# Attention over 16 images: the order of the outputs changed, and the setup rearranged

## The reference, cut to what matters

```python
xn = group_norm(x, gamma, beta)               # 32 groups, over an image's 1024 tokens
xf = xn.reshape(B, N, C)                      # B 16, N 1024, C 512
q = xf @ wq + bq
k = xf @ wk + bk
v = xf @ wv + bv
scores = jnp.einsum('bnc,bmc->bnm', q, k) * C ** (-0.5)
attn = jax.nn.softmax(scores, axis=-1)
out = jnp.einsum('bnm,bmc->bnc', attn, v)
out = out @ wp + bp
return out.reshape(B, H, W, C) + residual     # residual is x
```

## Time and profile before

| | |
|---|---|
| median of three runs | 2138.52 us |
| the profiled execution | 2139.97 us, of it 2138.3 us from the first to the last instruction |
| PE busy | 2099.0 us (98%) |
| DVE busy | 1798.7 us (84%) |
| POOL busy | 877.3 us (41%) |
| ACT busy | 743.7 us (35%) |
| one image inside the loop | 129.78 us |

### The profile page before, as it was taken

The page is one execution under the profiler, slowest core; times in us unless marked ns, Lnnn a source line. Parts: engine busy times, 40 slices in busy tenths (PEclk is TensorE's granted clock), DMA queues, the critical chain, the costliest instruction groups (busy, mean ns, idle before and its releaser), DMA issues.

```text
span 2138.3 us, 28427 instructions
## 1 busy us (share of the span) xinstructions
PE 2099.0 (98%) x9253; PEld 1730.9 (81%) x9253; DVE 1798.7 (84%) x2554; ACT 743.7 (35%) x1216; POOL 877.3 (41%) x475
## 2 busy tenths in 40 slices
PE   7999999999999999999999999999999999999999
PEld 5877888888888888888888788888878888888887
DVE  6898897988979888888888979889788898888865
ACT  4242332423333243332523324233332433335232
POOL 2452442524335244443524425243352434435253
PEclk9999999999999999999999999999999999999999
DMA  8003012030300203012030120303012030120101
GB/s 211 20 11 109 1 54 64 15 103 0 94 24 34 83 0 118 0 49 69 10 108 0 56 62 15 103 0 93 25 34 83 0 118 0 49 69 10 69 1 60
DMA packets 110268, 108.13 MB, mean 51 GB/s; under 512 B 8476, under 2 KB 74016, under 8 KB 110240
## 3 DMA queue, kind: packets, MB, share of 16 engines
q1 hardware_dynamic: 107984, 103.58, 16.0%
q10 hardware_dynamic: 2256, 4.20, 0.8%
HBM read 74.19 MB, written 33.55 MB: 50 GB/s over the span
## 4 chain that ended last, share of the span: by engine, by line
PE 51%; DVE 19%; issue 18%; POOL 7%; ACT 3%; DMA 0%; POOLq 0%; DVEq 0%; ACTq 0%
PE psum L1226 6%; PE psum L1228 6%; PE psum L1227 6%; PE psum L1251 5%; PE psum L1253 5%; PE psum L1252 5%; PE psum L1140 4%; PE psum L1139 4%; PE psum L1137 4%; DVE pt_lo L694 4%; POOL total_part L449 4%; DVE score L869 3%; DVE xn_lo L694 3%; POOL total_part L458 2%; PE psum L1057 2%
## 5 line engine op out<-in xcount | busy, mean ns | idle before, releaser
L1251 PE MATMUL psum<-v_hi,pt_hi 128*128 128x512 f32 x1024 | 401.4, 392 | 20.6 <-DVE pt_lo L694 17.4
L426 POOL TENSOR_TENSOR x_res<-x_res,out_bias 128x512 f32<-128x512 f32 x128 | 201.8, 1600 | 499.1 <-PE psum L1140 371.4
L1252 PE MATMUL psum<-v_lo,pt_hi 128*128 128x512 f32 x1024 | 399.2, 390 | 0.0
L1253 PE MATMUL psum<-v_hi,pt_lo 128*128 128x512 f32 x1024 | 399.0, 390 | 0.0
L694 DVE TENSOR_TENSOR pt_lo<-score,pt_hi 128x512 fp32r<-128x512 f32 x256 | 295.2, 1178 | 28.3 <-POOL total_part L449 25.0
L449 POOL TENSOR_TENSOR total_part<-total_part,score 128x512 f32<-128x512 f32 x192 | 309.1, 1610 | 16.6
L592 ACT ACTIVATE score<-psum 128x512 f32<-128x512 f32 x256 | 152.5, 596 | 342.3 <-PE psum L1228 341.9
L1251 PEld LDWEIGHTS psum<-v_hi,pt_hi 128*128 128x128 f32 x1024 | 192.6, 188 | 68.5 <-DVE pt_lo L694 25.1
L1253 PEld LDWEIGHTS psum<-v_hi,pt_lo 128*128 128x128 f32 x1024 | 192.6, 188 | 40.3
L1252 PEld LDWEIGHTS psum<-v_lo,pt_hi 128*128 128x128 f32 x1024 | 192.7, 188 | 39.1
L1226 PE MATMUL psum<-v_hi,xn_hi 128*128 128x512 f32 x512 | 201.7, 394 | 0.0
(11 more groups left out here) (162 smaller groups left out, 3992.2 us busy)
## 6 DMA issues: line engine op xcount, KB each, us to landing
x_res<-in_x_dram SPq DMA_DIRECT2D x128, 256.0 KB, 3.0
out_dram<-x_res SPq DMA_DIRECT2D x128, 256.0 KB, 2.2
x_blk<-in_x_dram SPq DMA_DIRECT2D x240, 128.0 KB, 3.2
score<-in_x_dram SPq DMA_DIRECT2D x16, 128.0 KB, 8.0
w_q<-in_L_conv_wq_dram SPq DMA_DIRECT2D x1, 1024.0 KB, 5.5
w_k<-in_L_conv_wk_dram SPq DMA_DIRECT2D x1, 1024.0 KB, 7.9
w_v<-in_L_conv_wv_dram ACTq DMA_DIRECT2D x1, 1024.0 KB, 9.1
w_p<-in_L_conv_wp_dram ACTq DMA_DIRECT2D x1, 1024.0 KB, 13.0
```

Of the source, the lines that this page charges most:

```text
L426: last = nc.gpsimd.tensor_tensor(at, at, out_bias[:, first:end], ALU.add)
L1251: nc.tensor.matmul(dst, hi[:, m, queries], v_hi[:, m, :], start=m == 0, stop=False)
L1252: nc.tensor.matmul(dst, hi[:, m, queries], v_lo[:, m, :], start=False, stop=False)
L1253: end = nc.tensor.matmul(dst, lo[:, m, queries], v_hi[:, m, :], start=False, stop=m == NT - 1)
```

## The change

It has three parts, and it computes the same.

**The order of the outputs** (DVE, each image). The diagonal and reciprocal of the first half (`totals(b, 0)`) move from before the last lo part of the values to behind `shifts(b, 1)`. The loop over j no longer has the lo part of the next image's xn between the lo parts of the exponentials: it makes two lo parts and then output j, and all four `xn_lo_parts` follow. `variance(b + 1)` moves up from behind the last maximum to behind the seventh.

**Image 0.** POOL no longer adds the residual of tiles 0 to 3 (`first_residual` on DVE does it), and the lo parts of the four block sums move from behind the norm of image 1 to between the last four outputs; PE waits for them in the queries of image 1.

**Setup.** The loads of wv and wp are issued when wq has arrived, before ACT's first splits. The last quarter of image 0 is transposed ahead of wv's lo part. The variance comes ahead of two lo parts and of the bias sums (`sum_products`), which now stand between the lo parts of m. POOL's block sums stand behind the power and wait for the first half of xn; ACT splits them after the first queries. The first queries of image 0 use PSUM banks 0 to 3 in order (`first_bank(h, j)`), so that the first two needn't wait for the lo part of m.

```diff
-        def first_bank(j):
-            return work[(2 + j) % 4]
+        def first_bank(h, j):
+            return work[(2 * h + j) % 4]
...
             pool.wait_ge(s_seth, SET_A_LAST + 1)
+            root(0)
+
+            pool.wait_ge(s_xl0, KC)
             block_sum(S1, a21, a22, ALU.add)
...
             block_sum(S4, a12, ab_sum[:, S2], ALU.subtract)
-            root(0)
...
                 top(b, 1)
-                if starts(b):
-                    for i in range(TH):
-                        residual(b, i)
                 totals(b, 1)
...
-            setup_hi_parts(SET_WQ, wq_t_hi)
+
+            act.wait_ge(s_wload[0], 16)
             load_rows(act, wv, w_v, s_wload[2])
             load_rows(act, wp, w_p, s_wload[3])
+            setup_hi_parts(SET_WQ, wq_t_hi)
...
-                act.wait_ge(s_as, len(SUMS))
-            for at in SUMS:
-                nc.scalar.activation(ab_hi[:, at], ab_sum[:, at], ACT.Copy).then_inc(s_abh, 1)
...
+                    act.wait_ge(s_as, len(SUMS))
+                    for at in SUMS:
+                        nc.scalar.activation(ab_hi[:, at], ab_sum[:, at], ACT.Copy).then_inc(s_abh, 1)
                 v_hi_part(b, 0)
...
+            def first_residual(i):
+
+                dve.wait_ge(s_bias, BIAS_STEPS)
+                dve.wait_ge(s_xr[i], 16)
+                at = x_res[:, i, :]
+                nc.vector.tensor_tensor(at, at, out_bias[:], ALU.add).then_inc(s_res, 1)
...
-            for n, (at, c, r) in enumerate(WHOLE):
+            for n, (at, c, r) in enumerate(WHOLE[:2]):
                 block_lo(at, n + 1, whole_block(c, r))
             group_variance(0)
-            dve.wait_ge(s_wide, 16 * 3)
-            dve.wait_ge(s_again[0], 16 * NI)
-            sum_products(0, KC)
+            for n, (at, c, r) in enumerate(WHOLE[2:]):
+                block_lo(at, n + 3, whole_block(c, r))
             variance(0)
...
-            setup_lo_parts(SET_M, m_hi, m_lo)
+            setup_lo_parts(SET_M, m_hi, m_lo, 0, 2)
+            dve.wait_ge(s_wide, 16 * 3)
+            dve.wait_ge(s_again[0], 16 * NI)
+            sum_products(0, KC)
+            setup_lo_parts(SET_M, m_hi, m_lo, 2, KC)
...
+                    if more and m == 6:
+                        variance(b + 1)
...
-                if more:
-                    variance(b + 1)
...
-                    if starts(b) and m == 4:
-                        for n, at in enumerate(SUMS):
-                            block_lo(at, len(WHOLE) + n + 1, ab_sum[:, at])
-                totals(b, 0)
                 v_lo_part(b, NT - 1)
                 tile_shift(b, 1)
                 shifts(b, 1, 0, NT)
-                tile_out(b, 0)
+                totals(b, 0)
+                if starts(b):
+                    for i in range(TH):
+                        first_residual(i)
+
                 for j in range(KC):
                     pt_lo_parts(b, 1, 2 * j, 2 * j + 2)
-                    if more:
-                        xn_lo_parts(b + 1, j, j + 1)
-                    if j:
-                        tile_out(b, j)
+                    tile_out(b, j)
+                if more:
+                    xn_lo_parts(b + 1, 0, KC)
...
                         sum_lo_part(b + 1, i - TH)
+                    if starts(b):
+                        block_lo(SUMS[i - TH], len(WHOLE) + i - TH + 1, ab_sum[:, SUMS[i - TH]])
...
+                        pe.wait_ge(s_abl, len(WHOLE) + len(SUMS))
                         pe.wait_ge(s_xsl, earlier(n) * 4 + 1)
                     block_product(BANK_6, S2, p, xs_hi, xs_lo, 1, 1)
```

More of the change, by code:

```diff
@@ L567, in first_query_hi @@
                 act.wait_ge(s_first, h * KC + j + 1)
-                nc.scalar.activation(t_hi[h][:, j, :], first_bank(j), ACT.Identity, bias=wk_bq[:, j:j + 1]).then_inc(s_th, 1)
+                nc.scalar.activation(t_hi[h][:, j, :], first_bank(h, j), ACT.Identity, bias=wk_bq[:, j:j + 1]).then_inc(s_th, 1)
             def queries(n):
@@ L619, in second_split @@
                     nc.scalar.activation(xn_hi[:, k, BANK:N], x_t[:, 1, k, :], ACT.Copy).then_inc(s_xh, 1)
-            setup_hi_parts(SET_WQ, wq_t_hi)
+            act.wait_ge(s_wload[0], 16)
             load_rows(act, wv, w_v, s_wload[2])
             load_rows(act, wp, w_p, s_wload[3])
+            setup_hi_parts(SET_WQ, wq_t_hi)
             setup_hi_parts(SET_WK, wk_t_hi)
-            setup_hi_parts(SET_A, a_full, 0, KC - 1)
-            setup_hi_parts(SET_WV, wv_t_hi)
+            setup_hi_parts(SET_A, a_full, 0, KC - 2)
             act.wait_ge(s_wload[3], 16)
@@ L629, in _ @@
                 nc.scalar.activation(wp_hi[:, k, :], w_p[:, k, :], ACT.Copy).then_inc(s_wph, 1)
+            setup_hi_parts(SET_A, a_full, KC - 2, KC - 1)
+            setup_hi_parts(SET_WV, wv_t_hi)
             setup_hi_parts(SET_A_LAST - (KC - 1), a_full, KC - 1, KC)
@@ L798, in first_query_lo @@
                 dve.wait_ge(s_th, h * KC + j + 1)
-                nc.vector.scalar_tensor_tensor(out=t_lo[h][:, j, :], in0=first_bank(j), scalar=wk_bq[:, j:j + 1],
+                nc.vector.scalar_tensor_tensor(out=t_lo[h][:, j, :], in0=first_bank(h, j), scalar=wk_bq[:, j:j + 1],
                                                in1=t_hi[h][:, j, :].bitcast(FP32), op0=ALU.add,
@@ L942, in _ @@
             quarter_transpose(0, 2)
+            quarter_transpose(0, 3)
             setup_lo_parts(SET_WV, wv_t_hi, wv_t_lo)
-            quarter_transpose(0, 3)
             token_stats(0, 1, 0, KC)
@@ L1104, in work_bank @@
                 elif what in (("v", 0, 0), ("v", 0, 1)) and starts(n):
-                    pe.wait_ge(s_tl, 3 + what[2])
+                    pe.wait_ge(s_tl, 1 + what[2])
                 elif not (before and starts(n)):
@@ L1187, in first_queries @@
                     if h and j < 2:
-                        pe.wait_ge(s_tl, j + 1)
+                        pe.wait_ge(s_tl, j + 3)
                     elif h:
                         pe.wait_ge(s_free, j - 1)
+                    elif j == 2:
+                        pe.wait_ge(s_setr, lo_rank(SET_M) + 1)
+                    elif j == 3:
+                        pe.wait_ge(s_setr, lo_rank(SET_M) + 2)
                     elif j == 1:
-                        pe.wait_ge(s_setr, lo_rank(SET_M) + 2)
-                    elif j == 0:
-                        pe.wait_ge(s_setr, lo_rank(SET_M) + 1)
+                        pe.wait_ge(s_seth, SET_A_LAST + 1)
                     for k in range(KC):
@@ L1206, in first_queries @@
                         hi, lo = (part[:, k % 2, chunk(j % 2)] for part in block_parts(at))
-                        nc.tensor.matmul(first_bank(j), hi, xn_hi[:, k, tokens], start=k == 0, stop=False)
-                        nc.tensor.matmul(first_bank(j), hi, xn_lo[:, k, tokens], start=False, stop=False)
-                        last = nc.tensor.matmul(first_bank(j), lo, xn_hi[:, k, tokens], start=False, stop=k == KC - 1)
+                        nc.tensor.matmul(first_bank(h, j), hi, xn_hi[:, k, tokens], start=k == 0, stop=False)
+                        nc.tensor.matmul(first_bank(h, j), hi, xn_lo[:, k, tokens], start=False, stop=False)
+                        last = nc.tensor.matmul(first_bank(h, j), lo, xn_hi[:, k, tokens], start=False, stop=k == KC - 1)
                     last.then_inc(s_first, 1)
@@ L1302, in _ @@
                 image(0, True)
-                pe.wait_ge(s_abl, len(WHOLE) + len(SUMS))
             if B > 2:
```

## The result

The changed kernel took 2226.78 us (median of four runs, 2223.4 to 2229.24), the kernel before 2138.64 us beside it (median of four too; one of its executions took 3012.9 us). The ratio is 1.0412, with a 95% interval from 1.0397 to 1.0426: 4.1% slower, where 2220 us or 3.8% had been forecast. The profiled execution of the change took 2223.4 us, 2221.7 of them its span.

A forecast was written before the change was run, and what follows sets the result against it. PE, busy 98% of the span, was taken as the bound, with DVE's chain setting the changed loop's length: 2139.97 + 84 (loop) + 2.3 (image 0) - 5.3 (setup) = 2221.0 us, less 1.45: 2220 us, 3.8% slower; range 2185 to 2250.

The forecast's parts named there:

- The configuring instruction: POOL, second half in the loop: comes 0.2 us after the late reciprocal, the addition 6.8 to 7.3 us after it.
- the smaller sum: Loop total with the skill's 6 us code load: delay 5.5 us instead of 6.6, the sum some 15 us smaller.
- Rival (a): POOL's 7 us run from the reduction's end whatever waits between, so no delay: 2121 us; chance 0.09.
- The loop's size: Fourteen images, each 6.0 us longer (5.4 to 7.1) through DVE's chain: +84 us, from 76 to 99.
- rival (d): The delay holds and PE's waits also lower its clock in every image, 1.9 us each: 2247 us; chance 0.12.
- the middle term: DVE's chain from POOL's addition to the next image's `v_lo`: 0.5 us longer, from 0.2 to 1.3.
- only reordered: The formerly interleaved part of DVE's chain was taken as no shorter; with output 0 now inside, 0.5 us was added.
- The norm: DVE in the loop: the earlier reduction runs beside a norm step, so the norm ends 1.9 us later.
- would give: Loop without the delay: the new order gains 1.05 us an image, 14.7 for 14 images; not subtracted from the forecast.
- rival (b): No delay, but the norm step is held until the reduction ends; the loop gains nothing: 2136 us; chance 0.03.
- Setup and image 0: Setup -5.3 us (-10 to 0), from waits gone less work given back; image 0 +2.3 us (0 to +4).
- at half of that excess: Setup: POOL's eight bias-chain steps slowed beside DVE, 1.66 us instead of 0.69 at worst; half taken, 4.4 us given back.

The follow-up runs named there:

- e11: Changed kernel with the two waits ahead of POOL's first addition swapped, the exponential's first, nothing added: 2134.12 us, ratio 0.9967.
- e10: Changed kernel plus a tiny POOL addition behind the wait for the reciprocal, with a second wait for something long over: 2226.97 us, ratio 1.04.
- e1: Changed kernel with the first half's diagonal and reciprocal put back ahead of the last lo part of the values: 2130.71 us, ratio 0.996.
- e8: Changed kernel with nine more query products on PE in each image from 1 on, ahead of the fourth, where PE waited: 2208.56 us, ratio 1.0323.
- e4: Changed kernel with outputs, reciprocal and variance in their old order, leaving only the setup and image 0 edits: 2131.05 us, ratio 0.9961.
- e2: Changed kernel plus a tiny POOL addition (128 x 4) between the second half's reduction and the wait for the reciprocal: 2134.42 us, ratio 0.9979.
- e5: Changed kernel, reciprocal still late, with only the next image's variance put back behind the last maximum: 2229.76 us, ratio 1.0425.

## Why the prediction was right, point by point

**The configuring instruction.** It was forecast at 0.2 us behind the reciprocal and came there. The load was put at 6.8 to 7.3 us, and was 6.9. The pause of POOL was forecast as 16 us and was 15.62, that of DVE as 8 and was 8.56. The Trainium skill's 6 us for the first call behind a `ModifyPoolConfig` ("GPSIMD Engine Reference", "Instruction dispatch") fits in kind; here the first addition of the total came 6.7 to 7.7 us behind its configuring instruction in the loop (7.0 in the middle), and the rows decided rightly against the smaller sum. Rival (a), no delay at all, fell: the same compiled steps gave 15.6 us or 8.6 by the place of the wait (the change, e11), and e10 has 15.6 again.

**The loop's size.** Forecast +6.0 us an image, 84 in all. Measured from the third value tile of image 1 to that of image 15: 1904.96 us instead of 1817.07, so 87.9, or 6.28 an image. The forecast summed up DVE's chain. The parts as PE shows them were partly others:

| in an image | forecast | measured |
|---|---|---|
| output tile 0 waits for `v_lo` | 0.3 | 1.5 |
| output tile 4, `pt_lo`, more than the 1.4 before | 2.6 | 1.1 |
| queries, `v_lo` | 2.6 | 2.3 |
| lower clock behind that, mean | only in rival (d) | 1.3 |

The measured ones are the gaps between products in image 3 beyond the usual 0.227 us, the restart of 0.1 included, and the clock's 1.5 us in 12 images of 14. They make 6.2. The forecast's own parts make 5.5, half a us short of its 6.0. The wait in the queries stands ahead of the fourth query product; the prediction called it the third.

The 6.0 itself came from DVE's chain, and images 4 and 14, where the clock stayed up, show what that chain cost alone:

| term | forecast | measured, images 3 and 4 |
|---|---|---|
| POOL's addition later | 6.6 | 6.7 |
| DVE's work from there to the next `v_lo` | +0.5 | -0.6 |
| slack ahead of that `v_lo` | -1.1 | -1.2 |
| image longer, clock up | 6.0 | 5.0 (134.82 and 134.91 us, less 129.79) |

So the middle term was mis-sized, and the chain by itself came out under the lower bound of 5.4. The prediction took the `xn_lo` for "only reordered". In the kernel before, two of the four stood beside POOL's additions and took 2.31 us each; in the change all four come behind them and take 4.62 together, 2.2 us saved, against 0.8 more for the `pt_lo`, 0.7 for output 0 and 0.1 for the row term (before, then the change):

```profile
546.71 2.31 DVE L694 TENSOR_TENSOR xn_lo<-x_t,xn_hi 128x1024 fp32r<-128x1024 f32 x1
...
559.88 1.22 DVE L694 TENSOR_TENSOR xn_lo<-x_t,xn_hi 128x1024 fp32r<-128x1024 f32 x1
```

```profile
572.15 4.62 DVE L696 TENSOR_TENSOR xn_lo<-x_t,xn_hi 128x1024 fp32r<-128x1024 f32 x4
```

**The norm.** This step was mis-sized. It was to lose 1.9 us beside the reduction, by the one step of the earlier trace rows; it lost 3.2 (6.16 instead of 2.98), as three of the four steps were hit (2.77, 1.29 and 1.52 us instead of 0.81). The first reduction came 2.2 us sooner, not 1.8 (10.9 us behind PE's third value tile instead of 13.1), and the second fell into the norm as well. So the gain that the loop "would give", 1.05 us an image, was 0.1 (e1), though the sum didn't use it. Output tile 0 then waited as rival (b) had it, 1.2 us (1.5 with the restart). By its rule, for which the prediction named the Trainium skill ("SBUF — State Buffer", "Who interferes with whom"), a norm step is held until the reduction has ended. The trace doesn't agree: the second step, beside the first reduction from its start, ended at 538.64 and the reduction at 539.32, much as in the earlier trace rows, and the fourth ran from 539.78 to 541.30, wholly inside the maximum's reduction (539.24 to 541.97).

**The clock.** Rival (d), with a chance of 0.12 and 1.9 us an image, was in part what happened: 1.5 us in 12 images, 18 us (e8). The prediction gave the clock nothing in the loop. That the size of the loop came out right (6.28 for 6.0) is luck: the clock's 1.3 us an image, left out of the sum, and the 1.0 us by which DVE's chain was put too long nearly cancelled. The mechanism, the late configuring instruction, is not luck: each of its signs came as forecast.

**Setup and image 0.** PE starts the first scores at 70.98 instead of 77.23 us: 6.25 gained, 5.3 forecast. (The eight steps "at half of that excess" are 3.9 us and not 4.4, so the forecast's own terms give 5.8. The eleven experiments with this setup start the first scores between 70.33 and 72.50 us.) From there to the scores of image 1 it takes 137.40 us instead of 135.59: 1.8 lost, 2.3 forecast. The wait for `ab_lo` was 5.2 us for 6, and the clock fell behind it. The four residual steps on DVE took 5.80 us together, 1.8 each but for the first, beside POOL's additions. e4 puts both parts together at -8 us. It has the residual steps and the late lo parts of the sums too, but the old order of the outputs, and its image 0 is 2.3 us shorter than before: so the loss of image 0 comes with the new order.

**The sum.** 2138.3 + 87.9 - 6.25 + 1.8 = 2221.7 us, the span. The profiled execution was 3.4 us under the median of its runs; the one before was 1.3 over its own. Instead of taking 1.45 us off, 3.4 had to be added: 4.8 of the 6.8 us by which the forecast is short.

## What to carry to other kernels

Where an engine must load code before its next step, look at what stands ahead of the configuring instruction in the compiled order: a wait there turns a load that hid beside other work into a load behind it. Of several waits before a step, put the one that ends last next to the step (or give it a step of its own), and read in the compiled order whether it is then attached behind the load; here swapping two lines was worth 93 us. And a move that gives one engine its result earlier must be followed to what it then meets: here the variance, with its reductions 2.2 us sooner, brought a reduction into the norm and cost all that the new order had won.

## What the runs showed of the hardware

**The load has a price of its own in each direction.** Behind its configuring instruction a plain step came after about 7 us whatever its size (128 x 4 in e2: 6.8 to 7.6 us in 16 cases, 7.1 in the middle; 128 x 512, line 449, in the loop of the change: 6.7 to 7.7, 7.0 in the middle). A reduction came sooner, after 5.5 to 6.4 us, 5.7 in the middle (46 cases in the change).

**The clock falls behind quite short waits, not always.** In the change, 2.1 us without a product in the queries were followed by the lower clock in 12 images of 14 and not in two, with waits of the same length (2.05 us in image 3, 2.12 in image 4). In e10, with waits as long, it fell in all 14, in e5 in 12, but there images 8 and 11 were spared and not 4 and 14. In e1, where the loop's only waits from image 2 on are the 1.2 us at output tile 0, the clock stayed at 1.00 there. A wait of 1.6 us in the setup (before 31.70 us in e1, before 31.87 in the change) was followed by the lower clock in e1 and not in the change, the same products on either side:

```profile
30.00:38.00 8.00, 6.45 (x24) 5.13 (x24) 4.59 (x15) 1.20 (x2) 1.00 (x1) 0.79 0.91 197
```

```profile
30.00:38.00 8.00, 6.38 (x31) 5.14 (x30) 5.96 (x21) 1.32 (x3) 1.06 (x1) 1.00 0.89 186
```

Around the 5.2 us for `ab_lo` the clock fell too; over the 6 us behind that wait its mean was 0.69:

```profile
188.85:194.85 6.00, 6.00 (x19) 4.81 (x20) 2.25 (x4) 0.69 (x1) 0.00 (x0) 0.69 0.84 251
```

Why some waits are spared stays open.

**Filling a wait can pay.** In e8 idle PE time was filled with useless products, and the kernel gained 0.8% by it.
